# Expert jobs regrouped from ten to eight across both passes, and the second expert matrix fetched per slot

## The reference

```python
x = x + attn_a(layernorm(x))   # 16 heads of 8; shifted products, "attention" part
x = x + ffn(layernorm(x))      # pass 1 through the experts
x = x + attn_b(layernorm(x))   # the recurrence
x = x + ffn(layernorm(x))      # pass 2 through the same experts
```

```python
# attn_a, per head, shift(t, o) = t moved o steps later, zeros in front
gains = softmax(q @ W_qscale.T + scale_gain)                    # 11 scales
out = sum(gains[j] * D4[tau] * sum(q * shift(k, 2**j * tau)) * shift(v, 2**j * tau)
          for j in range(11) for tau in range(4) if 2**j * tau < 512)
out = out + softplus(bypass) * sum(q * k) * v
return (out * sigmoid(x @ W_gate.T + b_gate)) @ W_out.T + b_out

# attn_b
for t in range(512):
    h = tanh(h @ A.T + x[t] @ B.T);  y[t] = h @ C.T
return layernorm(y + x) * gamma + beta

# ffn, 8 experts, each token goes through one
e = argmax(x @ Wg.T)
return gelu(x @ W1[e] + b1[e]) @ W2[e] + b2[e]                  # 128 -> 512 -> 128
```

## Time and profile before

| | |
|---|---|
| median of 3 runs | 1466.86 us |
| lowest, highest | 1463.73, 1468.23 us |
| the profiled execution, its own time | 1461.65 us |
| its span in the trace | 1459.9 us |
| TensorE, busy | 1129.1 us (77%) |
| VectorE, busy | 830.6 us (57%) |
| GpSimd, busy | 771.3 us (53%) |
| ScalarE, busy | 674.4 us (46%) |
| mean granted TensorE clock | 0.87 of full speed |
| moved by DMA | 112.01 MB, mean 77 GB/s |

### The profile page before, as it was taken

The page is one execution under the profiler, slowest core; times in us unless marked ns, Lnnn a source line. Parts: engine busy times, 40 slices in busy tenths (PEclk is TensorE's granted clock), DMA queues, the critical chain, the costliest instruction groups (busy, mean ns, idle before and its releaser), DMA issues.

```text
span 1459.9 us, 32432 instructions
## 1 busy us (share of the span) xinstructions
PE 1129.1 (77%) x9702; PEld 824.4 (56%) x9702; DVE 830.6 (57%) x1815; ACT 674.4 (46%) x2124; POOL 771.3 (53%) x1258
## 2 busy tenths in 40 slices
PE   3666647886898888988888898776998888886863
PEld 1233325554666555665555565666776677765753
DVE  4788797888677876897785778333022211313010
ACT  2233315544546544664545554344454554544431
POOL 2444475438836497467585463966416713354042
PEclk9677768998899979996879999997798798989997
DMA  4600011112111122112121112453233334434452
GB/s 125 178 1 0 1 47 50 52 54 87 51 42 54 40 66 64 52 49 71 47 83 41 46 47 62 123 144 98 90 96 101 101 88 112 115 99 132 135 154 68
DMA packets 121574, 112.01 MB, mean 77 GB/s; under 512 B 16148, under 2 KB 90685, under 8 KB 121405
## 3 DMA queue, kind: packets, MB, share of 16 engines
q1 hardware_dynamic: 110640, 92.46, 22.3%
q0 software_dynamic: 8192, 16.79, 3.8%
q10 hardware_dynamic: 2573, 0.69, 0.2%
HBM read 81.31 MB, written 28.57 MB: 75 GB/s over the span
## 4 chain that ended last, share of the span: by engine, by line
POOL 31%; PE 28%; issue 14%; DVE 13%; ACT 8%; DMA 2%; SPq 2%; ACTq 1%; DVEq 1%; POOLq 0%
POOL acc L679 10%; PE bank L1012 7%; POOL back L706 6%; POOL sorted_x L695 6%; PE bank L999 5%; POOL mom L644 5%; PE bank L1039 3%; DVE term L1196 2%; ACT hT L848 2%; DVE made L1167 2%; POOL rrs L644 2%; PE bank L906 2%; PE bank L965 1%; PE bank L938 1%; POOL prs L644 1%
## 5 line engine op out<-in xcount | busy, mean ns | idle before, releaser
L679 POOL TENSOR_TENSOR acc<-acc,term 128x512 f32<-128x512 f32 x219 | 288.5, 1317 | 63.3 <-DVE term L1196 44.5
L1012 PE MATMUL bank<-w,hT 128*128 x1584 | 274.9, 310 | 56.8 <-ACT hT L848 48.3
L999 PE MATMUL bank<-xTb,w1b 128*128 128x128 f32 x1584 | 278.8, 314 | 12.4 <-ACT xTb L836 7.2
L848 ACT ACTIVATE hT<-bank,b1T 128x128 f32<-128x128 f32 x792 | 233.1, 373 | 106.1 <-PE bank L999 100.9
L1012 PEld LDWEIGHTS bank<-w,hT 128*128 128x128 f32 x1584 | 230.2, 211 | 87.0 <-issue 80.6
L999 PEld LDWEIGHTS bank<-xTb,w1b 128*128 128x128 f32 x1584 | 236.6, 217 | 32.3 <-issue 12.2
L1303 DVE TENSOR_TENSOR ysb<-bank,b2bc 128x128 f32<-128x128 f32 x198 | 56.5, 286 | 294.1 <-PE bank L1012 279.3
L1196 DVE TENSOR_TENSOR term<-bank,V 128x512 f32<-128x512 f32 x251 | 168.3, 683 | 59.2 <-PE bank L965 36.1
L706 POOL DMA_INDIRECT back<-sorted_y,slot_i x128 | 128.7, 1006 | 126.3 <-issue 72.9
L1167 DVE SCALAR_TENSOR_TENSOR made<-bank,qkvb,K 128x512 f32<-128x512 f32 x251 | 176.0, 741 | 18.0 <-PE bank L938 8.7
L868 ACT ACTIVATE hid<-bank 128x16 f32<-128x16 f32 x512 | 93.7, 183 | 191.1 <-PE bank L1039 189.7
(11 more groups left out here) (160 smaller groups left out, 1629.8 us busy)
## 6 DMA issues: line engine op xcount, KB each, us to landing
w1b<-in_W SPq DMA_DIRECT2D x198, 256.0 KB
xsb<-sorted_x SPq DMA_DIRECT2D x198, 64.0 KB
sorted_y<-ysb SPq DMA_DIRECT2D x198, 64.0 KB
X<-in_x SPq DMA_DIRECT2D x64, 64.0 KB
out_x<-X SPq DMA_DIRECT2D x64, 64.0 KB
sorted_x<-K SPq DMA_DIRECT2D x10, 256.0 KB, 3.6
sorted_x<-xnj,slot_i POOLq DMA_INDIRECT x128
back<-sorted_y,slot_i POOLq DMA_INDIRECT x128
```

The source lines that it names most:

```text
L679: nc.gpsimd.tensor_tensor(acc[:], acc[:] if k > 1 else term[0][:], term[k % NTERM][:], ALU.add).then_inc(S["terms_added"], 1)
L848: last = nc.scalar.activation(tile(hT[u], c), tile(bank[4 + u], c), ACT.Gelu, bias=b1T[:, ds(e * HC + c, 1)])
L999: last = nc.tensor.matmul(tile(bank[4 + n % 2], c), tile(w1b[n % W1_RING], c), xTb[n % 2][:], start=True, stop=True, skip_group_check=True)
L1012: last = nc.tensor.matmul(bank[4 + n % 2][:, 0:D], tile(hT[n % 2], c), w2[:, ds(e * (HC * D) + c * D, D)], start=(c == 0), stop=(c == HC - 1),
```

## The change

Three things change.

- **Jobs.** A job is now a list of units (pass, chunk), so that chunks of pass 1 and pass 2 share one job. There are eight: pass 1 of chunks 0 and 1; pass 1 of 2 to 6; pass 1 of 7 to 9 with pass 2 of 0 and 1; pass 1 of 10 to 13 with pass 2 of 2; pass 1 of 14 and 15 with pass 2 of 3 to 7; then pass 2 of 8 to 10, of 11 to 13, and of 14 and 15. They have 15, 27, 27, 27, 35, 19, 19 and 15 slots, 184 in all.
- **W2.** At the start W2 is loaded into the memory that later holds the normalised chunks, and written from there to a DRAM tensor `w2_rows` in which each expert's part is 128 rows of 2 KB. Each slot then loads its expert's part (256 KB, "loadv", ring of 3), on SyncE's queue, when the result matmuls of the slot three before are done. The result matmuls read this buffer at a fixed address, and TensorE's register work goes. The first normalisation waits for the DRAM copy (`w2_laid`).
- **Buffers.** Eight buffers for normalised chunks in place of four. The planner's assumed durations of "reduce" and "spread" are changed a little too.

```diff
-Job = namedtuple("Job", "phase first chunks tiles slots")
-
-
-def job(phase, first, chunks):
-    tiles = chunks * TPC
-    return Job(phase, first, chunks, tiles, tiles + NE - 1)
-
-
-JOB = [job(0, 0, 3), job(0, 3, 3), job(0, 6, 3), job(1, 0, 4), job(0, 9, 3), job(0, 12, 4), job(1, 4, 3), job(1, 7, 3),
-       job(1, 10, 4), job(1, 14, 2)]
+Job = namedtuple("Job", "units chunks tiles slots")
+
+
+def job(first, second=()):
+    units = [(0, c) for c in first] + [(1, c) for c in second]
+    tiles = len(units) * TPC
+    return Job(units, len(units), tiles, tiles + NE - 1)
+
+
+JOB = [job(range(0, 2), range(0, 0)), job(range(2, 7), range(0, 0)), job(range(7, 10), range(0, 2)), job(range(10, 14), range(2, 3)),
+       job(range(14, 16), range(3, 8)), job(range(16, 16), range(8, 11)), job(range(16, 16), range(11, 14)), job(range(16, 16), range(14, 16))]
...
-CHUNK_OF_PREP = [x.first + q for x in JOB for q in range(x.chunks)]
-PREP_OF = {(JOB[JOB_OF_PREP[p]].phase, CHUNK_OF_PREP[p]): p for p in range(PREPS)}
-W1_RING, X_RING, XN_RING = 3, 4, 4
+PASS_OF_PREP, CHUNK_OF_PREP = zip(*(u for x in JOB for u in x.units))
+PREP_OF = {u: p for p, u in enumerate(u for x in JOB for u in x.units)}
+W_RING, X_RING, XN_RING = 3, 4, 8
...
-            piece("PE", "reduce", i, b, [0, 0.85, 1.1, 1.4, 1.8][len(x)], USUAL,
+            piece("PE", "reduce", i, b, [0, 0.85, 1.0, 1.15, 1.35][len(x)], USUAL,
...
-            piece("PE", "spread", i, j, 1.0 if j == 0 or s.g == 2 else 0.45, USUAL,
+            piece("PE", "spread", i, j, 1.1 if j == 0 or s.g == 2 else 0.52, USUAL,
...
-        piece("SP", "loadw", s, 0, 0.3, rank, [("texp", n, 0), past("hidden", s - W1_RING, 1), past("loadw", s - 1)], lands=3.2)
+        piece("SP", "loadw", s, 0, 0.3, rank, [("texp", n, 0), past("hidden", s - W_RING, 1), past("loadw", s - 1)], lands=3.2)
+        piece("SP", "loadv", s, 0, 0.3, rank, [("texp", n, 0), past("result", s - W_RING, 1), past("loadv", s - 1), ("loadw", s, 0)],
+              lands=3.2)
...
-            piece("PE", "result", s, h, 0.68, rank, [("gelu", s, 1), ("result", s, 0) if h else None])
+            piece("PE", "result", s, h, 0.68, rank, [("gelu", s, 1), ("loadv", s, 0), ("result", s, 0) if h else None])
...
+        w2_rows = nc.dram_tensor("w2_rows", (NE * P, HC * D), F32, kind="Internal").ap()
...
+        w2b = [sb(f"w2b{u}", [P, HC * D]) for u in range(W_RING)]
...
-        xnj = [sb(f"xnj{u}", [P, CW]) for u in range(XN_RING)]
+        normal = sb("normal", [P, XN_RING * CW])
+        xnj = [normal[:, u * CW:(u + 1) * CW] for u in range(XN_RING)]
...
-            sp.dma_start(w2[:].rearrange("p (e c d) -> p e c d", e=NE, c=HC),
+            sp.dma_start(normal[:, 0:NE * HC * D].rearrange("p (e c d) -> p e c d", e=NE, c=HC),
                          a["W2"].rearrange("e (c p) d -> p e c d", p=P)).then_inc(S["w2_in"], 16)
-            sp.dma_start(b2bc[:], a["b2"].rearrange("e d -> (e d)").partition_broadcast(P)).then_inc(S["w2_in"], 16)
+            sp.dma_start(b2bc[:], a["b2"].rearrange("e d -> (e d)").partition_broadcast(P)).then_inc(S["b2_in"], 16)
+            sp.wait_ge(S["w2_in"], 16)
+            sp.dma_start(w2_rows.rearrange("(e p) x -> p e x", p=P),
+                         normal[:, 0:NE * HC * D].rearrange("p (e x) -> p e x", e=NE)).then_inc(S["w2_laid"], 16)
 
             for what, n, k in ORDER["SP"]:
                 if what == "loadw":
                     sp.wait_ge(S["tiles_ready"], JOB_OF_SLOT[n] + 1)
-                    if n >= W1_RING:
-                        sp.wait_ge(S["hidden_ready"], nth("hidden", n - W1_RING, 1))
+                    if n >= W_RING:
+                        sp.wait_ge(S["hidden_ready"], nth("hidden", n - W_RING, 1))
                     e = sp.value_load(te_i[:, n:n + 1], min_val=0, max_val=NE - 1)
-                    sp.dma_start(w1b[n % W1_RING][:], a["W1"][ds(e, 1), :, :].rearrange("a d h -> (a d) h")).then_inc(
-                        w1_in[n % W1_RING], 16)
+                    sp.dma_start(w1b[n % W_RING][:], a["W1"][ds(e, 1), :, :].rearrange("a d h -> (a d) h")).then_inc(
+                        w1_in[n % W_RING], 16)
+                elif what == "loadv":
+                    if n == 0:
+                        sp.wait_ge(S["w2_laid"], 16)
+                    if n >= W_RING:
+                        sp.wait_ge(S["y_psum"], nth("result", n - W_RING, 1))
+                    e = sp.value_load(te_i[:, n:n + 1], min_val=0, max_val=NE - 1)
+                    sp.dma_start(w2b[n % W_RING][:], w2_rows[ds(e * P, P), :]).then_inc(w2_tile_in[n % W_RING], 16)
...
+                        if n == 0:
+                            act.wait_ge(S["w2_laid"], 16)
...
-                    j = JOB_OF_SLOT[n]
-                    if j not in words:
-                        pe.wait_ge(S["w2_in"], 32)
-                        pe.wait_ge(S["tiles_ready"], j + 1)
-                        words[j] = packed_experts(pe, j)
-                    e = expert(words[j], j, n)
                     if k == 0:
                         pe.wait_ge(S["gelu_ready"], nth("gelu", n, 1))
+                        pe.wait_ge(w2_tile_in[n % W_RING], 16 * (n // W_RING + 1))
                     for c in (2 * k, 2 * k + 1):
                         last = nc.tensor.matmul(bank[4 + n % 2][:, 0:D], tile(hT[n % 2], c),
-                                                w2[:, ds(e * (HC * D) + c * D, D)], start=(c == 0), stop=(c == HC - 1),
+                                                tile(w2b[n % W_RING], c), start=(c == 0), stop=(c == HC - 1),
```

25 lines of the change are left out of this document (12 added, 13 removed).

## The result

The changed kernel takes 1461.98 us (median of 18 runs, 1458.76 to 1467.16), the kernel before in runs beside it 1468.28 us (18 runs). The ratio is 0.9964, 95% interval 0.9948 to 0.9981. The prediction was 1432 us; the measured gain is 5 to 6 us where it promised 35.

What follows compares the result with a forecast made beforehand. Attention on VectorE was taken to pace the earlier part, TensorE's slots and steps the tail. Span 126.6 + 509 + 292 + 481 + 20.5 = 1429, -10 registers, +5 loads: 1424, said as 1425, scaled to 1432 us; range 1395 to 1462.

Steps and rivals of the forecast that it cites:

- Attention's end, 928 us: End of the attention chunks: forecast at 928 us, where it ended at 949 before.
- step 2: Chunks 2 to 11 of attention, with 40 slots and 64 steps: 509 us, by VectorE's price.
- step 3: Chunks 12 to 15 of attention, with 37 slots and 176 steps: 292 us, the middle of 280.5 and 302.7.
- TensorE's price alone, 302.7: Chunks 12 to 15: 25.6 us per chunk, 3.44 per slot and 0.415 per step give 302.7 us.
- The jobs, -31: Whole span with fewer slots, otherwise spread: stretches summing to 1429 us, against 1459.9 before.
- The registers, -10: Result matmuls on TensorE: fixed W2 addresses remove register instructions between wait and matmul, saving 10 us.
- the bound: Upper limit of the register saving on TensorE: 99 waits x 0.29 us = 28 us.
- I leave the hole out: Tail behind attention: the old tail's missing 16 us will not recur, as steps and slots alternate at once.
- my prices: After attention, 3.44 us per slot and 0.415 per step; inside attention, 1.25 per slot and 0.23 per step.
- The loads, +5: SyncE's queue and the DMA engines: one more load per slot costs 5 us, bounds 0 and +25.
- The third rival: W2 loads come late through SyncE's list or the engines: 0.76 us per slot, 140 us, time 1572; chance 0.12.
- gains and losses cancel: Whole kernel: attention unchanged and +15 us for the loads, giving 1461; chance 0.03.

Runs made afterwards that it cites:

- e15: Changed kernel with the planner's old durations of reduce and spread; 1480.84 us, 1.0096 of the kernel before.
- e9: Changed kernel with the ten old jobs, W2 loads and eight buffers kept; 1488.01 us, 1.0174 of the kernel before.
- e10: Changed kernel with the ten old jobs and only the first three W2 loads, all of expert 0; 1464.18 us, 1.0006 of the kernel before.
- e11: Kernel before, result matmuls reading expert 0's W2 at a fixed address without register work; 1448.31 us, 0.9875 of the kernel before.
- e6: Changed kernel with only the first three W2 loads, all of expert 0; 1439.38 us, 0.9815 of the kernel before.
- e16: Kernel before with nine new jobs of at most four chunks, W2 resident, registers, four buffers, old durations; 1442.06 us, 0.984 of the kernel before.
- e17: e16 with W2 loaded per slot and TensorE's register work gone; 1463.69 us, 0.9995 of the kernel before.
- e7: Changed kernel, each W2 load after the first three bringing 64 KB for 256, same instructions and waits; 1455.83 us, 0.9919 of the kernel before.
- e8: Kernel before plus one 256 KB DRAM-to-DRAM copy per slot on SyncE's queue, not waited for until the end; 1481.85 us, 1.011 of the kernel before.
- e4: Changed kernel with W2 loads issued by ScalarE instead of SyncE; 1.0233 of the kernel before, on a slower chip.
- e18: e16 with the change's durations of reduce and spread; 1462.32 us, 0.9958 of the kernel before.
- e14: e10 with the planner's old durations of reduce and spread; 1451.85 us, 0.9915 of the kernel before.
- e13: e10 with four buffers of normalised chunks in place of eight; 1462.29 us, 0.9976 of the kernel before.
- e12: Changed kernel with pass 2 of chunk 7 moved from job 4 to job 5; 1469.97 us, 1.002 of the kernel before.
- e2: Kernel before, result matmuls reading one expert's W2 at a fixed address without register work, on a slower chip; 0.9793 of the kernel before.

## Why the prediction was wrong, point by point

**The chain of ratios.** Parts added one at a time, each at its ratio times 1466 us: the registers' work taken away, 0.9875 (-18 us); eight buffers, the copy at the start and the loads' places, 0.9915 (+6, within the two intervals); the durations, 1.0006 (+13); the new jobs, 0.9815 (-28); the loads, 0.9964 (+22). Sum -5 us. I had -31 for the jobs, -10 for the registers, +5 for the loads, nothing for the rest. Against that the loads came out 17 us dearer, the durations 13, the buffers and the copy 6 and the jobs 3, and the registers 8 us cheaper: 31 us, the distance from forecast to result within rounding. The parts do not simply add, though; each holds for the place in the chain where it was measured, as the durations show below.

- **Attention's end, 928 us: right** (929), in part by luck. Chunks 2 to 11 took 502 us for the 509 of step 2, and chunks 12 to 15 took 301 for the 292 of step 3: two misses that cancel. In step 3 TensorE's price alone, 302.7, was right, and taking the middle was not. The start held (first normalisation at 95.9 us, as before).
- **The jobs, -31: right in sum,** -28 without loads and -31 with them, but only with the durations that the change has. With the old ones the changed kernel is at 1.0096 (e15), and the old jobs would be at 1.008 if their loads cost what e9 and e10 show (0.9915 + 0.0168): the regrouping would bring nothing.
- **The registers, -10: too small,** 18 us measured. The mechanism was right: the 0.29 us per wait are gone. I took a third of the bound, and the waits were 62, not 99 (e11).
- **"I leave the hole out": wrong.** Behind attention, 929 to 960 us hold 3 slots and 19 steps, and 1038 to 1077 us 8 slots and 7 steps: 31 us for 18 by my prices, 39 for 30. Together 22 us, more than the 16 of before. They have different causes. In the first TensorE had the work that its list promised and ran it at half the clock, some 9 of the 13 us; prices taken from stretches at 0.88 and 0.94 do not hold there. In the second the steps were missing. Steps and slots alternate on TensorE's list, but a list does not say that the steps' chunk is ready. I had looked for the slots' dependencies alone, not for the recurrence's: chunk 10 needs a job of 27 slots to be gathered whole.
- **The loads, +5: the step that failed most.** 22 us. I read "1.52 us for two" as 0.76 each and left out the register read ahead of the first; I looked whether each load had its lead, and it had; and I did not sum SyncE's list for a slot. It is 3.55 us without an output store and some 3.99 with, above the 3.44 us that a slot took. The third rival had the mechanism but priced it as added to every slot. In truth little is paid while steps run beside the slots (e6 and the changed kernel stay within 5 us of each other until 1300 us), and most of it behind. The sign that I had named for that rival, TensorE waiting for `w2b` hundreds of times, did not show: there are 4 such waits, 8.1 us in all. SyncE's own waits show it. One row of mine spoke against me already: a W1 was 3.38 us late among slots alone, though I wrote that no row shows such a wait.
- **The durations: not costed.** I called them "changed a little". They move 12 to 19 us either way.
- **The number 1461** stands among my rivals (gains and losses cancel, 0.03) and inside my range (up to 1462). That is luck: that rival had attention unchanged and 15 us for the loads, and attention did end 20 us earlier.

What is shown of the step that failed, and what is not: that the loads cost some 22 us is shown by taking them away (e6, and e10 beside e9; in e16 beside e17 it is at least that). That it is neither their bytes nor the clock is shown in the last stretch (e7, e8, e9 beside e10). That it is SyncE's list is read from its waits: in the 100 us that end 10 us ahead of the last slot they are 0.9 to 6.4 us in every kernel that loads W2 on SyncE, and 18 or more in every kernel that does not, e8 with its copies (8.3) aside. No run gave SyncE room and left everything else alone; e4 comes nearest.

The Trainium skill (DMA: Bandwidth & Descriptors, "Anatomy of one DMA") says that a semaphore wait takes place on the issuing sequencer, ahead of the dispatch. The traces agree: the issue of a store starts only when VectorE's addition is done, and 21.3 us of such waits turned into 0.2. Its 2.0 us fixed and 0.6 us of moving are fitted to DMAs that GpSimd issues, while these loads are SyncE's. By the 0.6 us I had put 110 us, an estimate for a load that every slot waits for; they decided nothing here, as with a quarter of the bytes most of the cost stayed (e7).

**A tail in numbers.** The table takes from each trace the end of attention and the last slot, and prices TensorE's list between by the prediction's 3.44 us per slot and 0.415 per step.

| kernel | slots, steps | priced | measured | more |
|---|---|---|---|---|
| before (registers) | 111, 224 | 475 | 490 | 15 |
| e16 (registers) | 105, 224 | 454 | 467 | 13 |
| e18 (registers) | 109, 224 | 468 | 485 | 17 |
| e11 (neither) | 111, 224 | 475 | 480 | 5 |
| e6 (neither) | 107, 272 | 481 | 483 | 2 |
| e10 (neither) | 111, 224 | 475 | 488 | 13 |
| e14 (neither) | 109, 224 | 468 | 476 | 8 |
| e13 (neither) | 110, 224 | 471 | 476 | 5 |
| after (loads) | 107, 272 | 481 | 511 | 30 |
| e9 (loads) | 111, 224 | 475 | 506 | 31 |
| e17 (loads) | 105, 224 | 454 | 491 | 37 |
| e12 (loads) | 107, 272 | 481 | 521 | 40 |
| e15 (loads) | 114, 292 | 513 | 554 | 41 |
| e8 (registers and copies) | 111, 224 | 475 | 507 | 32 |

So the two prices carry over to other jobs and orders within some 10 us, where W2 comes in the same way. The surplus sorts by how it comes: 15 us with registers, 7 with neither, 36 with loads, on average. Each row is one trace, and the kernels with the eight jobs of the change have a lower granted clock over the span (0.83 to 0.84, for 0.86 to 0.87 with the ten), which the table does not take out. In the three pairs that differ in the durations alone, the slower one has the longer priced tail: e15 against the changed kernel 513 for 481, e18 against e16 468 for 454, e10 against e14 475 for 468. The sign agrees in all three, the size does not: 19, 17 and 13 us for 32, 14 and 7. Why a duration of 1.35 for 1.8 us leads the list to one order or the other stays open; with three pairs it may be chance which jobs it favours.

**What stays open.** What the wait for chunk 10's rows costs by itself; why the clock falls at 934 us; why copies that nobody waits for cost 15 us ahead of the last step (e8); whether output stores on another queue would give the loads room; and the new eight jobs with W2 resident, which were not tried, as SBUF does not hold W2 and the seven buffers that a job of seven chunks needs.

## What to carry to other kernels

Before adding a transfer per iteration, sum the whole list of the engine that issues it, for one iteration of the tightest stage, with the register reads that no issue's own time shows; lead and bandwidth did not show it here, and the engine's own waits (25.7 us of 100 before) are the slack to spend. A gain in one stage of a list-scheduled kernel is to be judged by what it leaves for the last stage: in e15 attention ended 20 us earlier and the whole took 19 us longer. A price per slot or step holds at the granted clock at which it was read; look at the clock of the stretch before calling a surplus a wait. And an edit that only changes a planner's numbers is an edit like any other; test it apart.

## What the runs showed that I had not expected

- A matmul whose address is formed in registers starts 0.34 us behind what it waited for, one with a fixed address 0.05 us (e11): 18 us over 198 slots on one chip, 31 us on a slower one (1552.79 to 1521.89).
- With TensorE busy for 22.8 of 24 us, the granted clock stood at 0.50 of full speed all the while (934 to 958 us of the changed kernel).
- A transfer of 256 KB per slot that nobody waits for, with no register read, costs 0.08 us per slot (e8, 16 us over 198), with register read, wait and consumer 0.12 (22 us over 184). The two fall in different places: the first ahead of the recurrence's last step, the second behind it.
- A load of a weight takes SyncE 0.35 us by its record and 1.1 to 1.5 us of its list.
- The same kernel took 1552.79 us on one chip and 1464 to 1469 on the others. With e2's edit, in one trace of each, attention ended 7 us later on the slow chip (955 us for 948) and the tail behind it took 543 us for 480; why was not found.
